# Graph attention layer with a small network per node: five of twelve node chunks moved into the edge stage, the rows that two edge groups share kept apart

## What is computed

```python
h = leaky_relu(layernorm(x) @ W.T + b)                   # N x 512, 8 heads
e = leaky_relu(e_src[src] + e_dst[dst])                  # per edge and head
a = exp(e - segment_max(e)[dst]) / segment_sum(...)[dst] * dist
x = x + segment_sum(h[src] * a, dst)                     # the edge part
y = layernorm(x)                                         # the node part
# per node: decode four one-hot nibbles of y, run two three-layer networks of width 160,
# round and clip two results, place one-hot digits in columns 128 to 159 and a carry in 160
x = x + ffn(y)
```

## Time and profile before

| | |
|---|---|
| times of three executions | 1625.12, 1619.53, 1617.17 us, median 1619.53 us |
| the profiled execution | 1627.28 us, span 1625.5 us |
| granted TensorE clock over the span | 0.897 |
| PE / DVE / ACT / POOL busy | 83% / 66% / 28% / 58% of the span |
| DMA | 200 GB/s, 67% of the 16 engines' time |
| projection, edges, nodes | until about 230 us, until 1431 us, from 1434 us |

### The profile page before, as it was taken

One profiled execution on the slowest core, in us unless ns is written; L12 is line 12 of the kernel. 1 busy time (PEld: TensorE's weight loads), 2 busy tenths in 40 slices (PEclk: granted clock), 3 DMA queues, 4 the chain that ended last, 5 costly groups with the idle time before them and its releaser, 6 DMA issues. The chain is left out here.

```text
span 1625.5 us, 20898 instructions
## 1 busy us (share of the span) xinstructions
PE 1345.5 (83%) x6231; PEld 871.8 (54%) x6231; DVE 1068.9 (66%) x2638; ACT 449.6 (28%) x1005; POOL 936.2 (58%) x1010
## 2 busy tenths in 40 slices
PE   7999713888888888888888888788888888969996
PEld 3344302666666666666666656565656666733332
DVE  3888833866657566656656677578576665648862
ACT  5567501111111111111111111211111111148884
POOL 3667755666666566666666666566666666134430
PEclk9999955999999899989899989889989989979998
DMA  6967555777777677767777777676667777365632
GB/s 218 294 206 244 182 155 154 203 204 209 202 228 238 193 203 203 211 200 210 204 203 207 218 212 213 190 241 198 199 199 205 207 203 203 93 220 205 232 125 83
DMA packets 146300, 325.85 MB, mean 200 GB/s; under 512 B 41336, under 2 KB 41720, under 8 KB 146180
## 3 DMA queue, kind: packets, MB, share of 16 engines
q0 software_dynamic: 62720, 208.78, 45.6%
q1 hardware_dynamic: 83460, 115.65, 21.3%
HBM read 268.12 MB, written 56.24 MB: 200 GB/s over the span
## 5 line engine op out<-in xcount | busy, mean ns | idle before, releaser
L173 POOL DMA_INDIRECT gathered<-table_h,k_src x784 | 745.5, 951 | 444.1 <-issue 212.8
L1025 PE MATMUL bank<-gathered,member 128*128 128x260 f32 x3136 | 804.9, 411 | 75.8 <-issue 74.1
L1025 PEld LDWEIGHTS bank<-gathered,member 128*128 128x128 f32 x3136 | 625.0, 203 | 266.2 <-issue 150.0
L939 DVE TENSOR_TENSOR gathered<-gathered,bank 128x512 f32<-128x512 f32 x784 | 478.4, 680 | 3.8
L1057 ACT ACTIVATE summed<-bank 128x520 f32<-128x520 f32 x112 | 67.7, 604 | 942.3 <-PE bank L1025 826.8
L895 DVE TENSOR_TENSOR member<-bank,k_rel 128x896 f32<-128x896 f32 x112 | 121.4, 1087 | 122.0 <-PE bank L1025 111.9
L520 PE MATMUL bank<-k_x_ahead,xT 128*128 128x512 f32 x392 | 172.8, 602 | 6.8 <-DMA xT<-in_xT 5.9
L1009 PE MATMUL bank<-w_ident,member 128*128 128x128 bf16 x784 | 74.5, 227 | 121.8 <-issue 52.5
L902 DVE TENSOR_REDUCE at_dst<-bank 128x56 f32<-128x168 f32 x112 | 36.8, 328 | 205.0 <-remote 203.5
L330 POOL TENSOR_TENSOR k_agg_ahead<-hrow,w_both 128x512 f32<-128x512 f32 x98 | 123.6, 1284 | 76.5 <-DVE edst L366 53.2
L1041 PE MATMUL bank<-summed,carried 128*1 128x260 f32 x444 | 133.6, 421 | 18.0 <-issue 17.4
(11 more groups left out here) (167 smaller groups left out, 986.9 us busy)
## 6 DMA issues: line engine op xcount, KB each, us to landing
table_agg<-summed SPq DMA_DIRECT2D x112, 260.0 KB
table_h<-hrow SPq DMA_DIRECT2D x49, 260.0 KB, 2.2
xt<-in_x SPq DMA_DIRECT2D x49, 256.0 KB, 4.1
xT<-in_xT SPq DMA_DIRECT2D x49, 256.0 KB, 4.3
gathered<-table_h,k_src POOLq DMA_INDIRECT x784
out<-gathered SPq DMA_DIRECT2D x12, 1024.0 KB, 4.9
k_agg_ahead<-table_agg SPq DMA_DIRECT2D x7, 1040.0 KB
k_x_ahead<-in_x SPq DMA_DIRECT2D x6, 1024.0 KB
```

The costliest lines, as they stand in the source:

```text
L173: pool.indirect_dma_start(out=keep["gathered"][:, g % SLOTS, j, :], out_offset=None, in_=t["h"][:, :], in_offset=bass.IndirectOffsetOnAxis ...
L939: nc.vector.tensor_tensor(values, values, by_half(coef[:, j * HEADS:(j + 1) * HEADS]).unsqueeze(3) .to_broadcast([P, 2, HEADS // 2, HD]), ...
L1025: last = nc.tensor.matmul(sums_of(g)[:, a, :], member[:, g % M, j, :], gathered[:, g % S, j, a * HALF:(a + 1) * HALF], start=start, stop=stop)
```

## The change

What it does:

- The carried row is gone from PE. A group's window is now 121 columns wide (`COLS`), rows 1 to 120 are stored as before, row 0 goes to a tile of shared rows in SBUF, and what `table_agg` held of that node is read back beside it. Eight parts of shared rows are added on DVE (`whole_shared`) and written back by an indirect DMA of POOL (`put_shared`); the last part comes when all groups are done.
- Seven chunks instead of two have their `front` in the edge stage, beginning 12 rounds after groups 35, 48, 58, 67, 74, 81 and 87.
- Five of them are done there wholly: the network's 13 steps run two a round, in one PSUM bank, over seven rounds each, from 19 rounds after the same groups; DVE chooses nets, computes the values and places digits (POOL and DVE did so in the node stage), and SP stores the results. The node stage begins at chunk 5.
- PE's order in a round: transposes, sums of tiles 0 and 1, a step, tile 2, the look-up matmuls of group u + 2, tiles 3 and 4, a step, tiles 5 and 6. The look-up moves from three rounds ahead to two, the transposes and members from five to four.
- To make room: 5 gather slots instead of 6, 6 member buffers instead of 8, 3 of transposed members instead of 4, one PSUM bank of looked-up shifts instead of two.
- The general branch is now also taken when a window is wider than 121, when two groups from the second on begin at one node, or when a chunk's nodes are not complete at its group.

The diff, cut to its core:

```diff
-SLOTS = 6
+SLOTS = 5
...
-AHEAD = 2
...
+AHEAD = 7
+WHOLE = 5
+COMPLETE = (35, 48, 58, 67, 74, 81, 87)
+SHARED = tuple(zip((1,) + COMPLETE, COMPLETE + (GROUPS,)))
...
-        M = 8
+        M = 6
         T = 4
+        K = 3
...
-            return psum[:, 2 * (g % 2):2 * (g % 2) + 2, 0:HALF]
+            return psum[0:COLS, 2 * (g % 2):2 * (g % 2) + 2, 0:HALF]
...
-            return psum[:, 5 if g % 2 else 7, 0:GROUP * PARTS]
+            return psum[:, 5, 0:GROUP * PARTS]
...
                 def store(g):
                     base = base_of(g)
                     if g >= 1:
-                        sp.wait_ge(s_put[(g - 1) % Q], 16 * ((g - 1) // Q + 1))
+                        i, at = part_of(g)
+                        sp.wait_ge(s_put[(g - 1) % Q], stored(g - 1))
+                        if g == SHARED[i][0] and i >= 2:
+                            sp.wait_ge(s_back, 16 * (i - 1))
+                        sp.dma_start(shared_before[at:at + 1, :], t["agg"][bass.ds(base, 1), :]
+                                     ).then_inc(s_put[g % Q], 16)
                     sp.wait_ge(d["evac"], g + 1)
-                    sp.dma_start(t["agg"][bass.ds(base, P), :], summed[:, g % Q, :]).then_inc(s_put[g % Q], 16)
+                    if g >= 1:
+                        sp.dma_start(t["agg"][1:, :][bass.ds(base, REACH), :], summed[1:COLS, g % Q, :]
+                                     ).then_inc(s_put[g % Q], 16)
+                        sp.dma_start(shared[at:at + 1, :], summed[0:1, g % Q, :]).then_inc(s_put[g % Q], 16)
...
                 for g in range(EARLY_GROUPS, GROUPS):
                     gather_group(pool, t, keep, g, None if g < S else (
                         lambda j: wait_alone(pool, d["sums"], (g - S) * GROUP + j + 1, s_pool_on)))
+                    for i in range(len(SHARED) - 1):
+                        if g == SHARED[i][1] + PUT_SHARED:
+                            put_shared(i)
+                put_shared(len(SHARED) - 1)
...
                 for u in rounds(5, 0):
                     stage(u, scores)
                     stage(u + 1, look_up)
-                    stage(u + 5, make_member)
+                    stage(u + 4, make_member)
                     stage(u, messages)
+                    for i in range(len(SHARED) - 1):
+                        if u == SHARED[i][1] + ADD_SHARED:
+                            whole_shared(i)
                     front(u)
+                whole_shared(len(SHARED) - 1)
...
-                    for j in range(GROUP - 1):
+                    for j in range(GROUP):
                         pe.wait_ge(d["msg"], g * GROUP + j + 1)
-                        add_tile(g, j, j == 0, False).then_inc(d["sums"], 1)
...
+                        add_tile(g, j, j == 0, j == GROUP - 1).then_inc(d["sums"], 1)
+                        if j == 1:
+                            unit_step(g, 0)
+                        if j == 2:
+                            stage(g + 2, at_edges)
+                        if j == 4:
+                            unit_step(g, 1)
...
-                for u in rounds(5, 1):
-                    stage(u + 3, at_edges)
-                    stage(u + 5, transpose)
-                    stage(u - 1, add_carried)
+                for u in rounds(5, 0):
+                    if u < 0:
+                        stage(u + 2, at_edges)
+                    stage(u + 4, transpose)
                     stage(u, add_up)
...
                     stage(u, exps)
                     stage(u - 2, evacuate)
-                    stage(u + 4, turn_member)
+                    stage(u + 3, turn_member)
                     front(u)
+                    unit_steps(u)
```

```diff
+                    elif n <= 10:
+                        g = n - 7
+                        part = slice(REM * g, REM * (g + 1))
+                        pe.wait_ge(fin["h2"], 5 * c + g + 1)
+                        nc.tensor.matmul(step_bank, w2[:, g, :], units[:, g, :], start=True, stop=False)
+                        nc.tensor.matmul(step_bank, w2[part, 4 + g, :], units[part, 4, :], start=False, stop=True
+                                         ).then_inc(s_block, 1)
```

More of the change, by code:

```diff
@@ L291, in _ @@
                         sp.dma_start(keep["node_no"][:, :], t["node_no"]).then_inc(s_nodes, 16)
-                        with nc.allow_non_contiguous_dma(reason="one column of node numbers"):
-                            sp.dma_start(keep["node_col"][:, :], t["node_no"][0:1, :].rearrange("o p -> p o")
-                                         ).then_inc(s_nodes, 16)
+                        with nc.allow_non_contiguous_dma(reason="columns of first nodes"):
+                            for i, (lo, hi) in enumerate(SHARED):
+                                sp.dma_start(keep["base_of"][0:hi - lo, i:i + 1],
+                                             t["dst"][0:1, lo:hi, 0:1].rearrange("o g j -> g (o j)")
+                                             ).then_inc(s_nodes, 16)
                     if 6 <= u < 6 + DIST_PIECES:
@@ L977, in front @@
                 def front(u):
-                    for c in range(AHEAD):
-                        step = u - FRONT_ROUND - FRONT_STEP * c
-                        if step in (0, 1, 2, 3):
+                    for c, step in at_step(u, FRONT + 14, (0, 1)):
+                        if c < WHOLE and step == 0:
+                            dve.wait_ge(fin["flags"], c + 1)
+                            choose_nets(nc.vector, dve, keep, choice, c, 0, CHUNK)
+                            dve.wait_ge(s_outs, c + 1)
+                            net_values(nc, dve, keep, choice, last_spare, outs, c, 0, CHUNK)
+                        if c < WHOLE and step == 1:
+                            dve.wait_ge(fin["res"], done_by(c + 1))
+                            place_digits(nc, dve, keep, choice, last_spare, row(c), c, 0, CHUNK)
@@ L1091, in front @@
                                                      ).then_inc(fin["y"], 1)
+                        if step >= CHUNK + 2 and c < WHOLE:
+                            j = step - CHUNK - 2
+                            act.wait_ge(fin["y"], done_by(c + 1))
+                            nc.scalar.activation(row(c)[:, j, :], row(c)[:, j, :], ACT.Identity,
+                                                 bias=offset[:, s, j:j + 1], scale=more[:, s, j:j + 1]
+                                                 ).then_inc(fin["res"], 1)
@@ new lines, in place_digits @@
+def place_digits(nc, dve, keep, choice, room, rows, c, s, k):
+    d, digits = keep["d"], keep["digits"]
+    active, active2 = choice["active"], choice["active2"]
+    rounded, hot, carry = (room[n] for n in ("rounded", "hot", "carry"))
+    done = TAIL_STEPS * c
+    dve.wait_ge(d["tail"], done + 7)
+    for j in range(k):
+        nc.vector.tensor_tensor(hot[:, j, :, :], digits[:, :, :], rounded[:, j, 0:2].unsqueeze(2).to_broadcast([P, 2, 16]),
+                                ALU.is_equal).then_inc(d["hot"], 1)
+    nc.vector.scalar_tensor_tensor(carry[:, 0:k], rounded[:, 0:k, 2], 0.5, active[:, s, 0:k], ALU.is_gt, ALU.mult
+                                   ).then_inc(d["tail"], 1)
+    for j in range(k):
+        place = rows[:, j, 128:160]
+        dve.wait_ge(d["hot"], tiles_to(c) + j + 1)
+        nc.vector.scalar_tensor_tensor(place, hot[:, j, :, :].rearrange("p a b -> p (a b)"), active2[:, s, j:j + 1], place,
+                                       ALU.mult, ALU.add).then_inc(d["placed"], 1)
+    dve.wait_ge(d["tail"], done + 8)
+    nc.vector.tensor_tensor(rows[:, 0:k, 160], rows[:, 0:k, 160], carry[:, 0:k], ALU.add).then_inc(d["tail"], 1)
```

439 lines of the change are left out of this document (283 added, 156 removed).

## The result

The changed kernel takes 1595.16 us (median of four, 1593.28 to 1601.94) against 1619.82 us before: a ratio of 0.9855, 95% interval 0.9821 to 0.9888. The forecast was 1588 us. The time came out as forecast, but most of the terms behind it did not: that the total fits is luck, as the last sections show.

The account below looks back on a forecast made before the run. PE was taken to bound the edge stage, losing 2.4 us of every round to clock and stops. 1627.3 - 67.5 + 9 + 18 + 5 + 4 = 1595.8 us profiled, less 7.8: 1588 us; 8-in-10 range 1500 to 1690.

Parts of the forecast that it names:

- the sign that I had named for being wrong: Edge stage: the forecast is wrong if step rounds exceed 13.5 us or plain rounds don't fall below 10.3.
- carried rows, 107 x 1.31: PE in the edge stage: 111 groups lose 0.96 us each, -107 us at full clock, scaled by 1.31 for stops.
- 121 columns, 44 x 1.31: PE's transposes: loading 121 columns of weights costs 0.4 us a round, 44 us, taken from bounds of 0 to 44.
- steps, 70 x 1.31, with DVE's 18 and ACT's 5: Edge stage: five chunks' network adds 70 us of PE, DVE's unhidden rows 18 us, ACT's late exponentials 5 us.
- the stops and dips are taken to grow with PE's work: 1.31: PE's edge-stage rounds: lost time scales with work, 10.32 / 7.86 = 1.31, turning +7 us of PE into +9.
- The fold's spacing: PE's transposes: 0.11 us apart, as where loading 128 columns outlasts the matmul behind it; the upper bound for 121 columns.
- The look-up at two rounds: Edge stage: DVE's 2.8 us after the look-up fits within PE's 4.3 us of tiles and transposes, 1.5 us to spare.
- Rival A: Edge stage: PE's stops shrink, 121 columns cost nothing (-58 us), DVE's rows hide (-18): 1512 us; 20%.
- Rival B: Step rounds: completions seen late stop everything, 35 x 2.85 = +100 us if half meet one: 1688 us; 27%.
- Rival C: Edge stage: the same waits at some 0.6 to 1 us a round cancel the gain, 1611 to 1627 us; 12%.
- Rival D: Whole kernel: the general branch is taken, much slower; 1%.
- The end of the edge stage: After group 111: store, DVE's addition and POOL's scatter before the first load of sums, +2 to +7, taken as +4 us.

Follow-up runs that it names:

- e1: The changed kernel without steps in the edge stage, two fronts there and the node stage from chunk 0: 1.0109 of the kernel before, 1653.5 us.
- e5: The kernel before with the two carried matmuls of each group left out, so shared nodes' sums lack a part: 0.9879 of the kernel before.
- e9: e3 with members, transposes and sums of 128 columns instead of 121, rows 1 to 120 stored as before: 1.0160 of the kernel before.
- e3: e2 with six gather slots, seven members, four transposed members, transposes and members five groups ahead: 1.0178 of the kernel before, 1662 us.
- e6: e3 without the two small DMAs a group for the shared row: 1.0046 of the kernel before.
- e2: e1 with a second bank of looked-up shifts and the look-up of group u + 3 right behind the transposes: 1.0122 of the kernel before.
- e4: The changed kernel with coefficients and node numbers in SBUF, a second bank of shifts, look-up of group u + 3 behind the transposes: 0.9822 of the kernel before.
- e8: The kernel before with six of seven gathers per group, from the seventh group on, replaced by one plain DMA of as many rows: 0.8276, 1341 us.
- e10: e8 with the carried matmuls left out as in e5: 0.7642 of the kernel before, 1249.5 us.

## Why the prediction was right or wrong

The forecast lay 7 us off only because large errors cancelled. That is luck, and the sign that I had named for being wrong (plain rounds that don't fall below 10.3 us) did appear. Term by term, ratios turned into us at 1620:

| term | forecast, us | measured, us | from |
|---|---|---|---|
| node stage, five chunks | -67.5 | -65.8 | last sum to end: 204.6 in e1, 138.8 after |
| carried rows, 107 x 1.31 | -140 | -20 | e5 |
| 121 columns, 44 x 1.31 | +58 | 0 | e9 against e3 |
| two small DMAs a group | 0 | +21 | e3 against e6 |
| rest of the sharing | +4 | +27 | e6 against e5 |
| shorter look-ahead, five slots | 0 | -11 | e1 against e3 |
| steps, 70 x 1.31, with DVE's 18 and ACT's 5 | +115 | +25 | -41 after against e1, less -65.8 |
| sum | -31 | -24 | |

The measured column adds up by its making: each row from e5 on is the next kernel against the one before it, and the node stage stands in two rows with opposite sign. Most of the -11 is the start, where e1's first sum comes 9.9 us before e3's.

**The step that failed** is "the stops and dips are taken to grow with PE's work: 1.31". A us of PE work was worth 0.18 us when it went out (e5), and some 25 / 70 = 0.36 or less when steps came in. The factor was an average, used as if it were a marginal price. The average was right (10.32 / 7.86), but its excess comes with the gathers, and PE's stops and a lower clock make up for most of what its work leaves: in e5 some 73 and 30 us of it. Both signs of PE's work were overrated, so removing 107 and adding 70 + 44 looked like +9 and measured near nothing too.

**The checks that I named.** The node stage: right, and a chunk takes 65.8 / 5 = 13.2 us. Sums from 274 to 1460 us: they ran from 259 to 1461. Rounds without steps 9.6 us: wrong, 10.7; this is the case that I had called being wrong. Step rounds 12.5: 11.4 in a stretch that is mostly theirs. POOL waited for PE's sums no less than before (170 against 149 us from 285 to 1400 us), so the gathers' own 8.7 us did not bound. Transposes 0.11 apart: wrong, seven start and the first sum follows within 0.40 us, where before it was 0.48:

```profile
410.14 0.57 PE L1132 MATMUL bank<-w_ident,member 128*121 128x128 bf16 x7
410.54 2.84 PE L1148 MATMUL bank<-gathered,member 128*121 128x260 f32 x12
```

A load of 121 columns does take longer, 138 ns against the 97 of the row below. The rule of the Trainium skill, "TensorE: Matmul & The Clock Gate", on weight-path perf modes, agrees with this. But seven transposes and what follows take no longer, e9 shows no cost, and the value at the other bound, nothing, was the right one. The fold's spacing was the wrong neighbour.

```profile
L1009 PEld LDWEIGHTS bank<-w_ident,member x784: 96/97/152, 232.1 to 1383.0; 128*128 128x128 bf16 x196
```

**The look-up at two rounds.** I checked it against messages alone ("it fits, with 1.5 us to spare"). The chain that broke was longer: look-up, members, messages, the next scores, the exponential, ACT's copy of members, then the transposes at the head of PE's round. Stops there grew by some 130 us, and those inside the stream fell by 62; e2 and e4 show that the place hardly matters. The chain is read from the order and from single timelines; no run took it apart.

**Rival A** had one part right, the free 121 columns, and its gain never came, since PE's work did not set the round. **Rival B** had its mechanism: late completions stop DVE, then PE, by up to 10.7 us. But it took them to be confined to step rounds and added to the rest. In fact the rounds without steps carry them as much (they last 10.7 us, not 9.6), and step rounds took 11.4 us, less than the forecast's 12.5 and not 2.85 more. Nor was the clock there below B's 0.88: it was 0.92, and 0.86 in the rounds without steps. **Rival C** had the same waits cancel the gain, at 1611 to 1627 us; the time came out below that. **Rival D** did not occur.

**The end of the edge stage** cost 12.4 us, not 4. From the last copy to the first load pass 15.8 us, before 3.4. POOL's scatter is issued by 1467.45, and every engine's first instruction of the node stage comes at 1477.1:

```profile
1461.40 0.60 ACT L1231 ACTIVATE summed<-bank 121x520 f32<-121x520 f32 x1 [5.53 <-PE bank L1148]
...
1464.80 0.69 DVE L1110 TENSOR_TENSOR shared<-shared,shared_before 25x520 f32<-25x520 f32 x1 [8.51 <-DMA shared<-summed]
1466.50 0.95 POOL L977 DMA_INDIRECT table_agg<-shared,k_base_of  x1 [37.12 <-issue]
1477.16 0.44 SPq L1565 DMA_DIRECT2D gathered<-table_agg  x1
```

**DMAs of SP** I had called free since their issue is. Their 21 us show that issue time is not the price of a small DMA in a stage whose DMA engines are some 70% busy; by which way they cost that was not tried.

**Open.** How an indirect DMA of POOL holds PE up. The stops come in steps of about 0.7 us (0.7, 1.4, 2.1), also within one fp32 matmul where no wait stands, and in clusters, in e3 often some 65 or 130 records of PE apart; in the same stream of e8 no two sums start over 0.62 us apart. That ACT's copies follow the end of POOL's first burst speaks for its issue rather than for the scattered rows, and e4, where they don't, leaves it open again; gathers of fewer bytes, or scattered loads that POOL does not issue, were not tried. Of the 27 us of "rest of the sharing", 12 are the end; the other 15 (the store of 120 rows, eight additions and scatters, seven members, the last tile in its own round) were not taken apart. Whether the clock falls because PE stops, or both come from the gathers, is open too: the two always came together.

## What to carry to other kernels

Before removing work from the engine that is "86% busy", price one us of it: leave some of it out, though the result then lacks it, and look whether the time follows. An average of lost time over work (here 1.31) is no marginal price when another engine's activity makes the loss. Where a kernel is full of stops that the profile puts down to nothing, replace the suspect (here indirect DMAs) by a plain stand-in of as many bytes: one run showed 280 us that none of the reorderings of PE tried here reached. And when a forecast comes true, measure its terms: here a sum of wrong ones came within 7 us.

## What the runs showed of the hardware

- With POOL's indirect DMAs come stops of PE, a lower clock and a late sight of its completions. With one in seven of them from the seventh group on, and as many bytes, the clock goes from 0.91 to 1.00, PE from 86% to 100% busy, the kernel from 1620 to 1341 us.
- While POOL issues them back to back, a finished PE step can stay unseen for over 20 us: in the kernel before, transposes that started at 245.99 us were copied by ACT at 270.17, 4.6 us after POOL's burst. In e4_look3, with coefficients and node numbers in SBUF, the copies at the start were not held up by such a burst (first sum at 238.9 us).
- Work left out of PE under gathers lowers its clock: 0.91, 0.87 and 0.84 from 300 to 1300 us in the kernel before, e5 and e3. Where PE stops, a us of its work is worth 0.18 us; where it hardly does (e8 against e10), 0.90 to 0.96.
- A DMA of one 2 KB row makes 14 packets; two for each of 111 groups cost 21 us. Storing 127 rows a group instead of 120 made the kernel 46% slower (2419 against 1662 us).
- bf16 weights of 121 columns load in 138 ns, of 128 in 97, and with matmuls of 128 columns between them the difference is not seen in the kernel's time (1.0178 and 1.0160 of before).
